# Convolution matmuls that stream one padded run of three rows, in place of four separate rows

## The reference

```python
x = x + _L0_conv_ref(_gn(x), L0_conv_weights, L0_conv_biases)   # 3x3, zero pads
x = x + _L1_conv_ref(_gn(x), 5)      # Newton-Schulz inverse of each 128x128 channel, 5 steps
x = x + _L2_conv_ref(_gn(x), L2_conv_weight)                    # 3x3, circular (by FFT)
x = x + _L3_conv_ref(_gn(x), L3_conv_K)   # 3x3, zero pads, last row and column masked to 0
```

## Time and profile before

| | |
|---|---|
| median of 3 runs | 697.55 us (696.89 to 698.51) |
| span of the profiled execution, first to last instruction | 696.2 us |
| the profiled execution's own time | not recorded; the median is 1.35 us over its span |
| mean granted TensorE clock | 0.974 of 2.4 GHz |
| TensorE busy | 621.8 us, 89% |
| VectorE busy | 543.7 us, 78% |
| ScalarE busy | 280.2 us, 40% |
| GpSimd busy | 198.3 us, 28% |
| convolution matmuls of 512 and of 256 columns | 1080 and 216 in the program |

### The profile page before, as it was taken

How to read it: one execution, slowest core, us unless ns; L and a number is a source line. 1 busy time by engine, 2 the same in 40 slices (tenths; PEclk the granted TensorE clock), 3 DMA queues, 4 the chain that set the end, 5 groups by cost and what they waited for, 6 DMA issues and landing times.

```text
span 696.2 us, 13213 instructions
## 1 busy us (share of the span) xinstructions
PE 621.8 (89%) x4136; PEld 530.7 (76%) x4136; DVE 543.7 (78%) x1582; ACT 280.2 (40%) x489; POOL 198.3 (28%) x299
## 2 busy tenths in 40 slices
PE   0596895999999999999999999999999999989756
PEld 0365895889779887889779887889779887987544
DVE  3866788888998797988988798987998689478560
ACT  0252222534264345424255245534264345324432
POOL 6026223440424231340414231340423041211202
PEclk9998997999999999999999999999999999999888
DMA  5131033341325414441315414441314214400432
GB/s 153 50 92 43 16 79 115 78 127 53 108 69 122 121 47 116 111 126 49 118 52 124 120 38 124 112 125 49 117 53 93 76 44 126 102 31 33 128 97 61
DMA packets 82837, 60.85 MB, mean 87 GB/s; under 512 B 8238, under 2 KB 75982, under 8 KB 81870
## 3 DMA queue, kind: packets, MB, share of 16 engines
q1 hardware_dynamic: 78558, 54.80, 28.9%
q0 software_dynamic: 4224, 5.43, 3.1%
HBM read 23.46 MB, written 16.91 MB: 58 GB/s over the span
## 4 chain that ended last, share of the span: by engine, by line
PE 56%; DVE 17%; SPq 12%; issue 7%; DMA 5%; ACT 2%; DVEq 0%; POOL 0%; ACTq 0%
PE conv_ps L615 30%; PE V_ps L759 11%; SPq L285 10%; PE R_ps L752 9%; DVE st L553 4%; PE R_ps L704 3%; DVE d_A L503 2%; DMA x<-out_A 2%; DVE V L953 2%; DVE x L958 2%; DMA win_C<-rows_dram 1%; SPq L271 1%; DVE dev L568 1%; SPq L318 1%; DVE sums L895 1%
## 5 line engine op out<-in xcount | busy, mean ns | idle before, releaser
L759 PE MATMUL V_ps<-V,R 128*128 128x128 f32 x1280 | 171.5, 278 | 4.3 <-DVE V L953 3.8
L759 PEld LDWEIGHTS V_ps<-V,R 128*128 128x128 f32 x1280 | 156.8, 194 | 6.5 <-DVE V L953 3.1
L752 PE MATMUL R_ps<-R 128*128 128x128 f32 x1024 | 138.3, 279 | 5.9 <-DVE R L932 5.9
L752 PEld LDWEIGHTS R_ps<-R 128*128 128x128 f32 x1024 | 126.7, 195 | 6.4 <-DVE R L932 6.4
L825 ACT ACTIVATE R<-R_ps 128x512 f32<-128x512 f32 x128 | 76.3, 596 | 121.4 <-PE R_ps L752 121.2
L615 PE MATMUL conv_ps<-d_C,w_C 128*96 128x512 f32 (+1 forms) x486 | 113.8, 388 | 10.1 <-POOL d_C L648 3.9
L1128 POOL TENSOR_TENSOR U<-V,x 128x512 f32<-128x512 f32 x32 | 42.4, 1331 | 260.5 <-DVE V L953 260.5
L615 PEld LDWEIGHTS conv_ps<-d_C,w_C 128*96 128x96 f32 x486 | 74.9, 165 | 40.3 <-issue 6.1
L615 PE MATMUL conv_ps<-d_A,w_D 128*96 128x512 f32 (+1 forms) x432 | 99.5, 385 | 4.4 <-DVE w_D L496 3.9
L615 PE MATMUL conv_ps<-d_A,w_A 128*96 128x512 f32 (+1 forms) x378 | 88.2, 389 | 4.0 <-DVE d_A L503 4.0
L615 PEld LDWEIGHTS conv_ps<-d_A,w_D 128*96 128x96 f32 x432 | 66.8, 164 | 29.9 <-DVE w_D L496 4.0
(11 more groups left out here) (173 smaller groups left out, 736.3 us busy)
## 6 DMA issues: line engine op xcount, KB each, us to landing
win_C<-rows_dram SPq DMA_DIRECT2D x40, 256.0 KB, 4.0
rows_dram<-x SPq DMA_DIRECT2D x32, 256.0 KB
y<-out_D SPq DMA_DIRECT2D x160, 48.0 KB
win_D<-out_C SPq DMA_DIRECT2D x7, 1056.0 KB, 6.8
x<-out_A SPq DMA_DIRECT2D x139, 48.0 KB
win_A<-x SPq DMA_DIRECT2D x84, 64.0 KB
win_A<-x POOLq DMA_DIRECT2D x56, 64.0 KB, 3.0
win_D<-out_C SPq DMA_DIRECT2D x14, 160.0 KB, 5.8
```

Of the source, the lines that this page charges most:

```text
L752: ins = pe.matmul(R_ps[s][:, m, :], Rk[:, m, :], Rk[:, m, :], start=True, stop=True)
L759: ins = pe.matmul(V_ps[s][:, m, :], Rk[:, m, :], V[ch][:, m, :], start=True, stop=True)
```

## The change

The matmuls no longer go by `SPLIT_G` but by a second division `CONV_G` of the 22 windows: seven groups of three and one of one (`CG` = 8). A matmul reads one unbroken run of `d`, from the first of its rows to the last, with the two pads between neighbouring rows: 2 x 130 + 128 = 388 columns, or 128 for the last group. The pads give columns of the PSUM buffer that the eviction skips. All else still goes by `SPLIT_G`: `convs_of(g)` says how many matmul groups must be done for the windows of split group `g` (2, 3, 4, 6, 7, 8), `split_of(j)` which split group the last window of matmul group `j` lies in (0, 1, 2, 2, 3, 4, 5, 5). The work that stood behind the third, fourth, fifth group now stands behind the fourth, the sixth, the seventh. In `windows_from_windows` the load of D's windows waits for D's matmuls of the image before in place of its low parts.

```diff
+CONV_ROWS = 3
+CONV_G = [(k, min(CONV_ROWS, NBLK - k)) for k in range(0, NBLK, CONV_ROWS)]
+CG = len(CONV_G)
+PITCH = W + 2
...
+def convs_of(g):
+    return -(-(SPLIT_G[g][0] + SPLIT_G[g][1]) // CONV_ROWS)
+
+def split_of(j):
+    last_row = CONV_G[j][0] + CONV_G[j][1] - 1
+    return last_row // SPLIT_G[0][1]
...
         def rows_from_windows(eng, b, g, done=s_x1, first=0):
-            eng.wait_ge(cA.s_out, at(NG, b, g + 1))
+            eng.wait_ge(cA.s_out, at(CG, b, convs_of(g)))
...
         def windows_from_windows(sp, b):
-            sp.wait_ge(cC.s_out, at(NG, b, NG))
-            wait(sp, cD.s_dl, at(NG, b))
+            sp.wait_ge(cC.s_out, at(CG, b, CG))
+            wait(sp, cD.s_acc, at(CG, b))
...
-        TAIL = [(k0, k1, min(k1 // SPLIT_G[0][1] + 1, NG)) for k0, k1 in ((0, 9), (9, 18), (18, NBLK))]
+        TAIL = [(k0, k1, min(k1 // CONV_ROWS + 1, CG)) for k0, k1 in ((0, 9), (9, 18), (18, NBLK))]
...
         def store_y(sp, b, groups=range(NG), done=None):
-                wait(sp, cD.s_out, at(NG, b, g + 1))
+                wait(sp, cD.s_out, at(CG, b, convs_of(g)))
...
         def win_stats_1(dve, c, b, *parts):
-                        dve.wait_ge(cC.s_out, at(NG, b, (3 * j + 2) // SPLIT_G[0][1] + 1))
+                        dve.wait_ge(cC.s_out, at(CG, b, j + 1))
...
         def high_parts(act, c, b, g):
-                    act.wait_ge(cA.s_acc, at(NG, b + 2, g + 1))
+                    act.wait_ge(cA.s_acc, at(CG, b + 2, convs_of(g)))
...
         def conv_group(pe, c, b, g, prev, beside=False):
-            k0, kn = SPLIT_G[g]
+            k0, kn = CONV_G[g]
-            pe.wait_ge(c.s_dl, at(NG, b, g + 1))
+            pe.wait_ge(c.s_dl, at(NG, b, split_of(g) + 1))
             if c is cC:
-                pe.wait_ge(s_pad, at(NG, b, g + 1))
+                pe.wait_ge(s_pad, at(NG, b, split_of(g) + 1))
...
-            n = 0
+            n, cols = 0, (kn - 1) * PITCH + W
             for dx in range(TAPS):
                 for wp, dp in ((0, 0), (0, 1), (1, 0)):
-                    ins = pe.matmul(conv_ps[g % 2][0:OP, 0:kn, :], c.w[:, wp, dx * OP:(dx + 1) * OP],
-                                    c.d[:, dp, k0:k0 + kn, dx:dx + W], start=n == 0, stop=n == 8)
+                    run = c.d[:, dp, :, :].rearrange("p k w -> p (k w)")
+                    ins = pe.matmul(conv_ps[g % 2][0:OP, 0:cols], c.w[:, wp, dx * OP:(dx + 1) * OP],
+                                    run[:, k0 * PITCH + dx:k0 * PITCH + dx + cols], start=n == 0, stop=n == 8)
...
         def conv_out(act, c, b, g):
-            act.activation(c.out[:, k0:k0 + kn, 0:wn], conv_ps[g % 2][0:OP, 0:kn, 0:wn], ACT.Identity,
+            got = conv_ps[g % 2][0:OP, 0:kn * PITCH].rearrange("p (k w) -> p k w", w=PITCH)
+            act.activation(c.out[:, k0:k0 + kn, 0:wn], got[:, :, 0:wn], ACT.Identity,
...
         def pe_norms(pe, b, prev, nxt):
-                if g == 2:
+                if g == 3:
                     pe.wait_ge(s_abs, at(1, b, 1))
...
-                if g == 3:
+                if g == 5:
                     pe.wait_ge(s_dg, at(1, b, 1))
...
         def pe_cycle(pe, i, prev, nxt, nxt2):
-                if prev and nxt and g == 2:
+                if prev and nxt and g == 3:
                     win_mean(pe, cD, i - 1)
-                if prev and nxt and g == 4:
+                if prev and nxt and g == 6:
                     win_var(pe, cD, i - 1)
...
-                if g == 2:
+                if g == 3:
                     row_mean(pe, sC_bn, sC_sum, i)
-                if g == 3:
+                if g == 5:
                     row_var(pe, sC_bn, sC_sum, i)
...
         def act_norms(act, b, prev, nxt):
-                if nxt and prev and g >= 3:
-                    high_parts(act, cA, b + 1, g - 3)
+                if nxt and prev and g in (4, 5, 7):
+                    high_parts(act, cA, b + 1, (4, 5, 7).index(g))
...
         def act_cycle(act, i, prev, nxt, nxt2):
-                if nxt and prev and g == 4:
+                if nxt and prev and g == 6:
                     win_sqrt(act, cD, i - 1)
...
-                if g == 3:
+                if g == 5:
                     act_sqrt(act, sC_ve, sC_sd, tC[:, 3, :], tC[:, 2, :], i)
...
         @block.tensor
                 conv_group(pe, cA, 0, g, None)
-                if g == 2:
+                if g == 3:
                     win_mean(pe, cA1, 1)
-                if g == 3:
+                if g == 5:
                     win_var(pe, cA1, 1)
```

More of the change, by code:

```diff
@@ L195, in build @@
         scl = sb("scl", [128, 4, C])
-        conv_ps = [pb(f"conv_ps{i}", [128, 4, W]) for i in range(2)]
+        conv_ps = [pb(f"conv_ps{i}", [128, 512]) for i in range(2)]
         R_ps = [pb(f"R_ps{s}", [128, NMAT, 128]) for s in range(2)]
@@ L344, in windows_from_windows_last @@
             for (k0, k1, groups), s in zip(TAIL, s_tail):
-                sp.wait_ge(cC.s_out, at(NG, B - 1, groups))
+                sp.wait_ge(cC.s_out, at(CG, B - 1, groups))
                 sp.dma_start(w[C:C + OP, k0:k1, :], o[:, k0:k1, :]).then_inc(s, 16)
@@ L620, in conv_out @@
         def conv_out(act, c, b, g):
-            k0, kn = SPLIT_G[g]
-            act.wait_ge(c.s_acc, at(NG, b, g + 1))
+            k0, kn = CONV_G[g]
+            act.wait_ge(c.s_acc, at(CG, b, g + 1))
             if g == 0:
@@ L666, in build @@
         per_Vp = NCHK * STEPS
-        T_ps = [V_ps[0], V_ps[1], conv_ps[0], conv_ps[1]]
+        T_ps = [V_ps[0], V_ps[1]] + [conv_ps[j][:, :].rearrange("p (m w) -> p m w", m=NMAT) for j in range(2)]
         def n_R(r, k, s):
@@ L723, in pe_norms @@
             pe_gram(pe, b, 1)
-            for g in range(NG):
+            for g in range(CG):
                 if nxt and prev and g == 1:
@@ L1233, in _ @@
                 high_parts(act, cA1, 1, g)
-            for g in range(NG):
+            for g in range(CG):
                 conv_out(act, cA1, 1, g)
-                if g == 5:
+                if g == 7:
                     act_sqrt(act, sB_ve, sB_sd, tB[:, 3, :], tB[:, 2, :], 0)
```

26 lines of the change are left out of this document (14 added, 12 removed).

## The result

The changed kernel takes 719.58 us, the median of four runs (717.30 to 720.98), against 697.35 us (696.89 to 698.51) for the kernel before. The ratio is 1.030, with a 95% interval of 1.027 to 1.033. The predicted range of 702 to 719 us missed the median by 0.6 us; the predicted time of 711 us stood 8.6 us too low. The profiled execution took 720.98 us with a span of 719.3, so 1.7 us lie around the span.

What follows compares the result with a forecast made beforehand. No engine bounds the kernel throughout; hand-overs between engines set the time. Terms 5.2 + 3.0 + 3.3 + 1.3 + 0.8 + 0 gave +13.6 us: a span of 709.8, with 1.35 around it 711 us, range 702 to 719.

Steps and rivals of the forecast that it cites:

- Price of a matmul: On TensorE, a 388-column matmul taken at 173 ns (bounds 164 to 185), so a convolution goes from 11.70 to 11.66 us.
- the bound worked out by columns: On TensorE, if a matmul's excess goes by its columns, one run of 388 costs 180 ns.
- The rival of 185 ns a matmul: On TensorE, the whole excess belongs to each matmul whatever its shape: +23 us, 720 us; chance 0.12.
- Stores of A: SyncE's stores at L285 start later, since four windows need two matmul groups: +0.87 us in passes 1 to 6, +5.2.
- Both matmul buffers come free in time: TensorE never waits for evictions, as one (0.57 us) is much shorter than a matmul group; counted at nothing.
- Channel variance of C: L593 in convolution D waits for two groups, delaying VectorE's weights for C: +0.99 us over three jumps, +3.0.
- Boundaries without a jump: Passes 1 to 2, 5 to 6, 6 to 7: C's third group waits for later pads, +0.4 each, +1.3.
- Rest of C after its stall: More matmul work remains behind the stall before C's third group: +1.09 us in three passes behind a jump, +3.3.
- Norms: Norms transposed after four groups, spread after six: up to 1 us later for VectorE, but covered; counted at nothing.
- Start: The second image's variance moves from four groups to six, delaying the second convolution: +0.8 us.
- End: Last C's eviction and statistics end about 0.6 us sooner, last D's stores start about 0.6 us later: 0.
- the last boundary: The boundary from pass 6 to 7, without a jump: +0.4 us from C's third group waiting for pads.

Runs made afterwards that it cites:

- the two mends there: Two separate edits to the changed kernel: C's row variance issued one matmul group sooner (716.00 us); ScalarE's square root for B behind D's second eviction (716.56 us).
- The experiment with added work: Six unused 128x128 multiplications before C's third group in the loop's passes, added to the changed kernel with stores of A by matmul group (715.54 us): 711.55 us.
- the first seven experiments: Changed kernel with rows of 128; earlier variance; later square root; stores by group; those stores plus added multiplications; three mends together; eight regrouped matmul groups: 704.86 to 720.26 us.
- all nine kernels with runs or rows of three: The changed kernel (719.58 us), the first seven experiments, and the regrouped matmul groups with the three mends (702.57 us).
- the two others: Kernel before with first stores of A waiting for the second eviction (720.67 us); separate rows in groups of two or four windows with stores by matmul group (697.68 us).

## Why the prediction was right or wrong

**Direction and mechanism** were right: on TensorE's throughput the change is small, 0.24 us a convolution, and the hand-overs set the time. The size was not: +22.2 us by the medians against +13.6.

**Price of a matmul: row price taken, column price measured.** I took 173 ns "as four rows against two show most of the excess going with rows or columns, and a run has one start". It is 177.5, and the experiment with separate rows shows that a run of 388 and three rows of 128 cost alike; the bound worked out by columns, 180 ns, was the near one. The last group's matmuls start 85 ns apart, for the 84 taken. The Trainium skill's formula ("TensorE: Matmul & The Clock Gate", back-to-back issue gap), which gave 164 ns and which the page means for isolated matmuls, is off by 13 ns here. A convolution is then 7 x 9 x 177.5 + 9 x 84 = 11.94 us in place of 11.66, +0.3 us. It shows bare as the +0.3 of C to A in pass 1, and up to 1.9 us of that stretch's 6.7. The rival of 185 ns a matmul named 720 us, which is the measured time, by a price that doesn't exist: agreement of a total proves no mechanism.

**Stores of A** (+5.2, measured +6.1): right in place and nearly in size. 0.85 to 1.28 us a pass for 0.87. Undoing that lateness turned the stretch to -2.0, and delaying the stores of the kernel before shows one for one.

**Both matmul buffers come free in time: wrong.** I compared an eviction of 0.57 us with a group of 1.6 and didn't ask what stands between evictions on ScalarE. It is the square root for B, whose time VectorE sets; I listed the edits to the order, and this line had not been edited, but the groups around it had become shorter. 0.6 us in each of six passes, and with the longer matmuls D itself is 0.8 us longer. Putting it one eviction later won 3.0 us.

**Channel variance of C** (+3.0 behind jumps): the idle time at L591 (1.46 us, from 0.17) came as predicted, in every pass. But it is worth 0.4 us in each of six, 2.5 in sum, not 0.99 in each of three. The sum is near by two errors that cancel: the jump isn't what exposes it. The time between D and C has two paths of nearly one length, TensorE's late end of D and VectorE's late weights, and the two mends there gave 2.5 and 3.5 us of the 7.1.

**Boundaries without a jump** (+1.3): the wait that I worked out for C's third group is there (0.4 us in pass 2, 0.1 in pass 6, 0.3 in pass 7), and was the small part. D to C costs as much in them, 1.1 to 1.3, as behind a jump. I had put the D terms to the jumps alone, and that is the largest part of the miss: 7.1 for 3.0.

**Rest of C after its stall** (+3.3): in passes 4 and 5 1.10 and 1.66 us for 1.09. In pass 3 2.46, since behind the stall the clock was at 1.2 GHz for 3.4 us. The stall grew by 0.65, 0.83 and 1.35 us in the three passes, for the 1 to 2 I had named. "What TensorE saves before the stall it stands longer in it" was right, and I costed the standing at nothing. The experiment with added work shows the price, about 1.5 us each. The falls may make some of the spread from run to run as well: the fastest run of the changed kernel (717.30) has the highest mean clock, 0.976 against 0.971 in the others.

**Norms** (at nothing): VectorE's waits for the transposed sums and the spread norms grew from 5.0 to 13.3 us in all, but C to A grew by 0.31 us in pass 1, about what the matmuls of C are longer. The cover held.

**Start** (+0.8): +0.9, right. **End** (0, and 0.4 for the last boundary): +2.2. The clock falls several times behind 650 us in both kernels, and the part up to the last matmul (+1.4) lies between -1.4 and +0.8 in the first seven experiments; how much of it is the change stays open. The part behind the last matmul is not chance: it is +0.7 to +1.1 in all nine kernels with runs or rows of three, and 0.0 and -0.1 in the two others. The chain of the changed kernel ends with GpSimd's four stores of windows 16 to 19 (L386), which wait for seven groups and start 1.44 us before the last matmul ends, where before they start 2.17 ahead: 0.7 us later for the predicted 0.6. The 0.6 us that I had set against this, from the last C, lies before the last matmul, where these traces can't single it out.

## What to carry to other kernels

When a tile becomes smaller and its count larger, list every consumer that still goes by the old division, and every instruction that stands in a queue between two tiles, the unedited ones too: its cover was the length of the old tile. Price a longer stall of TensorE above its length, since the clock may fall behind it: in these runs 1.0 to 1.7 us each time. If the division must change, let the new borders fall on the old ones.

## What the runs showed of the hardware

- Matmuls of a run of 388 columns and of three rows of 128 at a distance of 130 start equally far apart, 177.5 ns, 16 over the 388 columns at 2.4 GHz; 512 columns in four rows are 22 over.
- Where a group of matmuls in a busy stream started 2.2 to 2.9 us behind the start of the matmul before it, the granted clock fell from 1.00 to 0.50 in 10 of 18 passes, for 3.4 us, and matmuls of 388 columns then started 321 to 325 ns apart. With six short multiplications (12 records) in the stall it stayed at 1.00 in three of three.
- The kernel before is nearer to this than its own trace tells: delaying the stores by 2 us brought four such falls into its stretches from A to D.
